# A decoder of six phases: the first pair's gathers at the start of the rotated heads moved ahead of the phase boundary

## What is computed

```
x = x + _L0_ffn_ref(_layernorm(x), ...)      # "mix": causal attention, then 8 experts, 2 per row
...
gates = softmax(x1 @ gate_w.T + gate_b)
_, top_idx = top_k(gates, 2)
expert_outputs = einsum('bsd,efd->bsef', x1, expert_w) + expert_b
moe_out = sum(sel * top_gates[..., None], axis=2)
return _layer_norm(x1 + moe_out, ln2_w, ln2_b)
...
x = x + _L1_attn_ref(_layernorm(x), ...)     # "rot": q and k through tanh layers and rotations
```

## Time and profile before

| | us |
|---|---|
| median of 3 runs (lowest, highest) | 3362.42 (3358.3, 3364.45) |
| the profiled execution, whole | 3364.29 |
| its span, first to last instruction | 3362.4 |
| mixed phase's last store, issue | 1194.56 |
| rotated heads' first instruction | 1198.15 |
| rotated heads' first matmul of rows (L2379) | 1211.6 |

### The profile page before, as it was taken

How to read it: one execution, slowest core, us unless ns; L and a number is a source line. 1 busy time by engine, 2 the same in 40 slices (tenths; PEclk the granted TensorE clock), 3 DMA queues, 4 the chain that set the end, 5 groups by cost and what they waited for, 6 DMA issues and landing times. The chain is left out here.

```text
span 3362.4 us, 71194 instructions
## 1 busy us (share of the span) xinstructions
PE 3202.7 (95%) x26568; PEld 2352.6 (70%) x26569; DVE 1772.9 (53%) x5682; ACT 1607.3 (48%) x3295; POOL 1494.3 (44%) x1990
## 2 busy tenths in 40 slices
PE   7998999998999779998999999999999999999998
PEld 5775566666777644444676777767777688999997
DVE  4666777765888556543455544554445565111114
ACT  4654666665666047884555445545455511111111
POOL 1002444433676146651665656655666564000017
PEclk9999999998999889999999999999999999999999
DMA  8700111100001650000000000000000013999963
GB/s 244 290 2 14 43 43 44 43 15 14 17 23 29 172 143 24 21 16 26 14 8 8 8 8 15 8 8 8 8 14 1 2 40 118 325 327 323 325 237 104
DMA packets 111490, 263.34 MB, mean 78 GB/s; under 512 B 24003, under 2 KB 70240, under 8 KB 95840
## 3 DMA queue, kind: packets, MB, share of 16 engines
q1 hardware_dynamic: 90208, 224.70, 21.0%
q0 software_dynamic: 16384, 26.29, 2.8%
q10 hardware_dynamic: 4608, 8.39, 0.7%
HBM read 196.61 MB, written 62.65 MB: 77 GB/s over the span
## 5 line engine op out<-in xcount | busy, mean ns | idle before, releaser
L3004 POOL TENSOR_SCALAR wide_probs<-wide_probs,wide_inverse 100x361 f32<-100x361 f32 x504 | 594.5, 1192 | 0.1
L3297 ACT ACTIVATE wide_probs<-wide_probs,wide_least 100x361 f32<-100x361 f32 x512 | 301.0, 592 | 6.8 <-DVE wide_least L3410 6.8
L3410 DVE CUSTOM_DVE_ANT_0 wide_probs<-banks,wide_bias 100x361 f32<-100x361 f32 x512 | 251.5, 529 | 42.8 <-issue 37.7
L3056 PE MATMUL banks<-w_wide_v,wide_c 64*120 64x512 f32 (+1 forms) x1152 | 266.0, 591 | 0.0
L3050 PE MATMUL banks<-wide_c,w_wide_k 64*128 64x361 f32 x1536 | 257.1, 467 | 2.3 <-PEq L4101 2.3
L2588 ACT ACTIVATE rot_h<-banks,w_rot_b 128x800 f32<-128x800 f32 x256 | 223.3, 923 | 54.7 <-PE banks L2414 49.1
L3002 POOL TENSOR_TENSOR wide_hold_pool<-eps 100x1 f32<-100x1 f32 x252 | 48.6, 193 | 444.7 <-DVE wide_inverse L3416 444.7
L3891 ACT ACTIVATE tiles_hT<-banks 128x512 f32<-128x512 f32 x114 | 68.1, 597 | 349.1 <-PE banks L3807 349.1
L3807 PEld LDWEIGHTS banks<-tiles_xT,tiles_w 128*128 128x128 f32 x1824 | 214.7, 194 | 4.7 <-issue 1.8
L3807 PE MATMUL banks<-tiles_xT,tiles_w 128*128 128x128 f32 x1824 | 215.3, 277 | 1.2 <-DVE tiles_xT L4053 1.2
L3050 PEld LDWEIGHTS banks<-wide_c,w_wide_k 64*128 64x128 f32 x1536 | 150.5, 188 | 90.8 <-issue 4.6
(11 more groups left out here) (499 smaller groups left out, 7173.2 us busy)
## 6 DMA issues: line engine op xcount, KB each, us to landing
tiles_w<-in_moe_w SPq DMA_DIRECT2D x114, 1024.0 KB, 5.2
slots<-zeros SPq DMA_DIRECT2D x58, 512.0 KB, 6.6
cross_c<-in_ctxT SPq DMA_DIRECT2D x32, 270.8 KB, 4.4
wide_c<-in_ctxT SPq DMA_DIRECT2D x32, 270.8 KB, 4.1
mix_kT<-slots SPq DMA_DIRECT2D x32, 256.0 KB, 4.3
slots<-mix_m_tiles_out ACTq DMA_DIRECT2D x32, 256.0 KB, 4.1
tiles_rows<-slots SPq DMA_DIRECT2D x57, 128.0 KB, 4.8
slots<-tiles_out SPq DMA_DIRECT2D x57, 128.0 KB, 5.0
```

The source lines that it names most:

```text
L3004: last = nc.gpsimd.tensor_scalar(t.probs[:, i, j, :], t.probs[:, i, j, :], t.inverse[:, i, j:j + 1], None, ALU.mult)
L3056: last = nc.tensor.matmul(make_bank(unit, lane)[0:kw, :], g.wide_c[rows_of(lane), of.buf, k, k0:k0 + kw], w.v[rows_of(lane), k, of.hf * BA ...
L3297: last = nc.scalar.activation(t.probs[:, i, j, :], t.probs[:, i, j, :], ACT.Exp, bias=t.least[:, i, j:j + 1], scale=-1.0, accum_out=t.rows ...
L3410: last = nc.vector.tensor_tensor_reduce(t.probs[:, i, j, :], scores(j), t.bias[:, :], -1.0, LARGEST, ALU.add, ALU.min, t.least[:, i, j:j + 1])
```

## The change

1. The four gathers of pair 0 leave GpSimd's head of the rotated heads. GpSimd issues them as its last instructions of the mixed phase, after waiting for the last store of each of the four ring places, into a buffer of its own, `first_got`.
2. On VectorE, the sums, statistics and centring of lane 0 come straight behind the tables; `base(0)` follows them.
3. The copies of the folded weights (with their waits) come behind the second statistics of pair 0, ahead of `apply_lane`; the halves of `w1` come behind `apply_lane`. PE waits for the halves (`halved`) before its first tanh layer.

```diff
@@ mix_phase, GpSimd
             tail()
+            for k in range(TILE_RING):
+                pool.wait_ge(rows_stored[k], 16 * (MIX_TILES // TILE_RING))
+            for lane in range(LANES):
+                for k in range(2):
+                    nc.gpsimd.indirect_dma_start(g.first_got[:, lane, k, :], None, g.slots[:, :],
+                                                 bass.IndirectOffsetOnAxis(ap=g.slot_i[:, 0, lane, k:k + 1], axis=0)).then_inc(g.lane_gathered[lane], 16)
@@ rotation_phase, GpSimd
             pool.wait_ge(g.loaded.rot, g.total.rot)
-            gather(0)
             root(m0, 0, 0)
@@ rotation_phase, TensorE, first_layer
                 if k == 0:
                     pe.wait_ge(s.k_kept, p + 1)
+                    if p == 0:
+                        pe.wait_ge(s.halved, 1)
@@ rotation_phase, VectorE
-            for e in range(2):
-                nc.vector.tensor_scalar(t.w1[:, e, :], w.w1[:, :], w.half[:, e:e + 1], None, ALU.mult)
-            dve.wait_ge(s.folded_ready, 1)
-            nc.vector.tensor_copy(t.w2[:, :, :, :], side[:, 0:DC * 2 * VROWS].rearrange("p (c e v) -> p c e v", e=2, v=VROWS))
-            nc.vector.tensor_copy(t.v_b[:, :], vec[:, 1:1 + DC])
-            nc.vector.tensor_copy(t.b2[:, :], vec[:, 0:1]).then_inc(s.folded, 1)
...
-            base(0)
             combine_lane(0, 0)
             centre(0, 0)
+            base(0)
             combine_lane(0, 1)
             finish(0, 0)
             centre(0, 1)
             stats_lane(0, 0)
             finish(0, 1)
             stats_lane(0, 1)
+            keep_folded()
             apply_lane(0, 0)
             apply_lane(0, 1)
+            halve_w1()
```

More of the change, by code:

```diff
@@ L2245, in rotation_phase @@
     with ExitStack() as ctx:
-        s = semaphores(nc, ctx, "rot", "fold_b masks picked own tables rot folded_ready folded turns whole_i whole near angle size cosine sine y yT_ready yT ybar mean_ready mean masked "
+        s = semaphores(nc, ctx, "rot", "fold_b halved masks picked own tables rot folded_ready folded turns whole_i whole near angle size cosine sine y yT_ready yT ybar mean_ready mean masked "
                        "k_ready k_kept q_ready q_kept kn_ready k_ends qn_ready spans inverse unit ratio rows_ready rows lane_ready proj_ready biased added "
@@ L2305, in gather @@
                     nc.gpsimd.indirect_dma_start(v.got[:, p % SETS, lane, k, :], None, g.slots[:, :],
-                                                 bass.IndirectOffsetOnAxis(ap=g.slot_i[:, p, lane, k:k + 1], axis=0)).then_inc(gathered[p % SETS] if p else lane_gathered[lane], 16)
+                                                 bass.IndirectOffsetOnAxis(ap=g.slot_i[:, p, lane, k:k + 1], axis=0)).then_inc(gathered[p % SETS], 16)
             def root(m, p, lane):
@@ L2683, in _ @@
             nc.vector.tensor_scalar(t.size[:, :, :], t.size[:, :, :], -1.0, float(np.pi / 2), ALU.mult, ALU.add).then_inc(s.size, 1)
-            for e in range(2):
-                nc.vector.tensor_scalar(t.w1[:, e, :], w.w1[:, :], w.half[:, e:e + 1], None, ALU.mult)
-            dve.wait_ge(s.folded_ready, 1)
-            nc.vector.tensor_copy(t.w2[:, :, :, :], side[:, 0:DC * 2 * VROWS].rearrange("p (c e v) -> p c e v", e=2, v=VROWS))
-            nc.vector.tensor_copy(t.v_b[:, :], vec[:, 1:1 + DC])
-            nc.vector.tensor_copy(t.b2[:, :], vec[:, 0:1]).then_inc(s.folded, 1)
-            dve.wait_ge(s.folded, 1)
-            dve.wait_ge(s.sine, 1)
-            dve.wait_ge(s.cosine, 1)
             def combine_lane(p, lane):
@@ L2702, in combine_lane @@
                 rows = v.sum[:, p % SETS, lane, :]
-                nc.vector.scalar_tensor_tensor(rows, v.got[:, p % SETS, lane, 0, :], g.coef[:, p, lane, 0:1], g.x1[:, b, :], ALU.mult, ALU.add).then_inc(s.half, 1)
+                got = v.got[:, p % SETS, lane, :, :] if p else g.first_got[:, lane, :, :]
+                nc.vector.scalar_tensor_tensor(rows, got[:, 0, :], g.coef[:, p, lane, 0:1], g.x1[:, b, :], ALU.mult, ALU.add).then_inc(s.half, 1)
                 dve.wait_ge(s.half, b + 1)
-                nc.vector.scalar_tensor_tensor(rows, v.got[:, p % SETS, lane, 1, :], g.coef[:, p, lane, 1:2], rows, ALU.mult, ALU.add).then_inc(s.summed, 1)
+                nc.vector.scalar_tensor_tensor(rows, got[:, 1, :], g.coef[:, p, lane, 1:2], rows, ALU.mult, ALU.add).then_inc(s.summed, 1)
                 dve.wait_ge(s.summed, b + 1)
@@ L2856, in step, with keep_folded, halve_w1 @@
                     ends_of_keys(k)
-            base(0)
+            def keep_folded():
+                dve.wait_ge(s.folded_ready, 1)
+                nc.vector.tensor_copy(t.w2[:, :, :, :], side[:, 0:DC * 2 * VROWS].rearrange("p (c e v) -> p c e v", e=2, v=VROWS))
+                nc.vector.tensor_copy(t.v_b[:, :], vec[:, 1:1 + DC])
+                nc.vector.tensor_copy(t.b2[:, :], vec[:, 0:1]).then_inc(s.folded, 1)
+                dve.wait_ge(s.folded, 1)
+                dve.wait_ge(s.sine, 1)
+                dve.wait_ge(s.cosine, 1)
+            def halve_w1():
+                for e in range(2):
+                    last = nc.vector.tensor_scalar(t.w1[:, e, :], w.w1[:, :], w.half[:, e:e + 1], None, ALU.mult)
+                last.then_inc(s.halved, 1)
             combine_lane(0, 0)
             centre(0, 0)
+            base(0)
             combine_lane(0, 1)
@@ L4184, in decoder @@
                 g[n] = rows_stack.enter_context(nc.sbuf_tensor("mix_" + n, shape, dt, side="right"))
+            g.first_got = rows_stack.enter_context(nc.sbuf_tensor("rot_first_got", [S, LANES, 2, D], F32, side="right"))
             mix_w["expert_b"] = weight_as(mix_stack, "mix_b", "mix_expert_b", [P, NE * D], i["mix_expert_b"].rearrange("e d -> (e d)").unsqueeze(0).broadcast_to([P, NE * D]))
```

## The result

Side by side on one chip, six runs each, the changed kernel takes 3372.91 us (3372.11 to 3377.85) and the kernel before 3363.36 us (3358.3 to 3364.45): a ratio of 1.0037, interval 1.0026 to 1.0048, so 8.7 to 16 us **slower**. The ratio, which isn't the quotient of the two medians, stands for 12.4 us; the medians themselves are 9.6 us apart (1.0028). The forecast was 3371.7 in a range of 3365 to 3376.

What follows compares the result with a forecast made beforehand. The bound was a chain of waits between mixed phase and rotated heads. Gathers 0.3 + 5.0, DRAIN 5.3, same barrier, less 0.2, gave + 10.4; less 1.15 in VectorE's head, + 9.25, a median of 3371.7 us, range 3365 to 3376.

Steps and rivals of the forecast that it cites:

- The gathers: Mixed phase's end on GpSimd: start 0.3 us after the last store lands (0.8 if slow), then 5.03 us, nothing hiding them.
- The DRAIN: GpSimd at the mixed phase's block end: paid in full behind the fourth gather, 5.3 us taken from 5.3 to 6.3.
- The rival in which it is free: Mixed phase's end: the DRAIN costs nothing, boundary 5.1 us, net + 4.0 us, time 3366.4 us; chance 0.15.
- The reason given: GpSimd's block ends: a block with indirect DMAs pays 5.3 to 6.3 us, however long ago they landed.
- The barrier: Between mixed phase and rotated heads: 1.4 us as before, VectorE starting 10.4 us later.
- all four terms: Boundary: gathers' start 0.3, gathers 5.0, DRAIN 5.3 and the same barrier, less 0.2 us, giving + 10.4 us.
- The head up to `rot_y`: VectorE's start of the rotated heads: shortened by 1.15 us, lane 1's `rot_y` 11.75 us behind the first instruction.
- The copies: VectorE ahead of `apply_lane`: 0.45 us, covered by lane 1's 0.49 us wait for GpSimd's root.
- the step "Nought": VectorE behind both lanes of `rot_y`: the products (0.61 us) moved there cost nothing.
- The cover named: VectorE behind `rot_y`: its 4.19 us wait for pair 1's rows hides the products; PE needs them 5.5 us later.
- The rival of a dip more or less: TensorE's clock after the boundary: one more or fewer drop moves the time 1.7 us, 3373.4 or 3370.0; chance 0.10.

Runs made afterwards that it cites:

- e7_waits: Changed kernel with no gathers at the mixed phase's end, GpSimd only waiting for the last stores there; one run, 3406.10 us beside 3400.41 of before.
- e3_nodrain_both: Changed kernel without GpSimd's DRAIN at the mixed phase's end and behind the clearing of semaphores; 3364.92 us over eleven runs, ratio 1.0007 to before.
- e3_nodrain_mix: Changed kernel without GpSimd's DRAIN at the end of the mixed phase's block only; 3375.34 us, ratio 1.0039 to before.
- e4_halves_front: Changed kernel with the two products of w1 back ahead of lane 0's sum; one run, 3406.32 us beside 3400.41 of before.
- e1_gathers_only: Changed kernel with VectorE's head back in its old order, only the gathers staying moved; 3374.62 us, 1.0039 times before.
- e2_head_only: Changed kernel with the four gathers back behind the barrier, VectorE's new order kept; 3366.87 us over ten runs, ratio 1.0011 to before.
- e9_two_over: Changed kernel without both GpSimd DRAINs, only lane 0's two gathers ahead of the boundary, products in front; 3396.17 us against 3393.88, ratio 1.0007.

## Why the prediction came out right, step by step

**The gathers.** They start 0.94 us behind the landing, where I took 0.3 and held 0.8 for the upper end: the bound was too low. From there to the end of the fourth it is 5.01 us (5.03 expected). Nothing hid them.

**The DRAIN.** The largest term, and the one that was only read from blocks in which it was off the path. It ended 5.62 us behind the last gather, inside the 5.3 to 6.3 given. The rival in which it is free (+ 4.0) falls with `e7_waits` (5.28 us with nothing queued), and with both DRAINs left out (`e3_nodrain_both`) the loss is gone. The reason given holds: a block with indirect DMAs pays, however long ago they landed, and `e7_waits` shows it with the scatters alone. Two things the forecast lacked: the price goes to whichever DRAIN comes first (`e3_nodrain_mix`), and it grows by 0.08 us with each indirect DMA, which is where the 0.3 above the 5.3 came from. That it needs indirect DMAs at all rests on the three blocks without them; no block was run with its own taken out.

**The barrier.** 1205.30 - 1203.94 = 1.36 us; 1.4 expected. With all four terms the boundary is 11.3 us longer than before; 10.4 was forecast, and 0.64 of the difference is the slow start, 0.3 the DRAIN.

**The head up to `rot_y`.** Better than forecast: lane 1's `rot_y` starts 10.94 us behind the first instruction instead of 11.75, a gain of 1.95 and not 1.15. The step that I had missed is the tables. I let them end as before, 3.54 us behind the first instruction, but they end at 3.08, which is 0.46 of the 0.80 us. (Most of the rest is in the joints between instructions: the sum of lane 0 starts 0.09 us ahead of the last table's end, and the additions hold lane 1's sum for 0.67 us and not 0.8.) Two small instructions on VectorE make most of the 0.46, beside gathers (kernel before) and without them (changed kernel):

```profile
1199.61 0.39 DVE L2668 TENSOR_SCALAR rot_turns<-rot_rot 128x8 f32<-128x8 f32 x1
...
1200.97 0.36 DVE L2679 TENSOR_SCALAR rot_angle<-rot_near 128x8 f32<-128x8 f32 x1
```

```profile
1206.71 0.17 DVE L2675 TENSOR_SCALAR rot_turns<-rot_rot 128x8 f32<-128x8 f32 x1
...
1207.81 0.17 DVE L2686 TENSOR_SCALAR rot_angle<-rot_near 128x8 f32<-128x8 f32 x1
```

**The copies** cost nothing, as said. In the changed kernel `rot_y` of lane 0 starts at 10.39 and lane 1's at 10.94, one 0.41 us instruction and a short wait for GpSimd's root behind it.

**The products behind `rot_y`.** Here the step "Nought" failed. The cover named was VectorE's wait of 4.19 us for pair 1's rows, and PE's weight load indeed did not wait for `halved` (1.37 us for `rot_q`, the same as in the earlier trace rows). But the wait is for gathers, and the products slowed the very gathers that VectorE then waits for: 3.05 us in place of 1.18, so 5.51 us of wait in place of 4.19. `e4_halves_front` takes the products away from there and the sum of pair 1 comes 1.28 us earlier. Of the 1.95 us won at `rot_y`, 0.10 are left at the sum of pair 1, and nothing at the 32nd tanh (63.64 us behind the first instruction, 63.62 before).

**What came through.** The two misses point the same way, and add up. The boundary costs 0.9 us more than forecast, and of the 1.15 us that the head was to give back, 0.1 are left at pair 1: + 11.2 by these landmarks, where + 9.25 was forecast. To the end of the span it is + 12.0, and the ratio stands for 12.4. The two medians happen to be only 9.6 apart, within the interval of 8.7 to 16. So it is luck that the time came out 1.2 us from the forecast; by its terms the forecast was 2 to 3 us too low. What it had right is the wait and its two large parts, the gathers in the open and the DRAIN behind them.

**The clock.** The rival of a dip more or less wasn't needed for the result, but its size can be read. TensorE's granted clock was 0.50 (1.2 GHz) from the gap until 16.0 us behind the first instruction and fell to that level twice more in the next 28 us; before, it was until 18.7, and twice. In `e1_gathers_only` it rose at 23.1 and never fell again. The prediction read the 0.88 after the gap as one such stretch that costs 1.7 us; there are two of 3.4 us each, so 0.12 of 28 us, 3.4 us, is already what they take from the clock together. The stretch from the 16th to the 32nd tanh shows what one of them is worth: 23.4 us in `e1_gathers_only` with none in it, 25.6 in the kernel before and 25.8 in the changed one with one of 3.4 us, 28.4 in `e2_head_only` with one of 6.8. A clock that differs like this from one kernel to the next moves the stage by 2 to 3 us, as much as everything that the head had to gain. It is also why I make no claim of time for `e4_halves_front`, a single run.

## What to carry to other kernels

Work moved ahead of a barrier to the engine that is done early is free only if the barrier does not wait for what that engine must still do at its end: add up its DRAIN too, even one that now ends over 70 us before the barrier (1120.75 against 1196.8 here). A price that is hidden in today's profile stands there all the same, in the row of the DRAIN against the end of the engine's last instruction. Here it is mostly the price of the 64 scatters, and GpSimd has 80 idle us behind them. In the kernel before, the DRAIN that follows the mixed phase's without new DMAs takes 47 ns (at 1197.9). So a DRAIN in the idle time would, by the 0.08 us a DMA, leave about 0.4 us to be paid behind the four gathers; that is an estimate from the table above and wasn't tried, and the 6 us until the gathers are through would stay. And before work is put into an engine's wait, ask what is being waited for, and whether the work slows just that.

## What was not expected of the hardware

- GpSimd's DRAIN at a block's end took 5.28 us with nothing queued and the last scatter over 80 us old (`e7_waits`). It grew by 0.08 us with each indirect DMA of the block (60: 4.98, 64: 5.30, 68: 5.63 us behind the last instruction) and was 0.07 us in blocks that had none. Left out at one block's end it was paid in full at the next one, 8.27 us from its begin, 5.6 behind the last gather.
- GpSimd's sequencer runs ahead of queued gathers only so far: with four of them it passed the block's end as the second started (1200.88 against 1200.85), with two 0.3 us after the first started (1198.68 against 1198.36).
- VectorE's instructions and GpSimd's gathers can slow each other: a gather took 3.05 us instead of 1.18 when VectorE's two products with four additions behind them ran beside it, in every profile in which they stood straight behind `rot_y`; and two of VectorE's 128x8 instructions took 0.36 and 0.39 us beside gathers instead of 0.17, while the others beside the same gathers kept 0.17 to 0.23. Why the products are harmless beside a gather at other places (1.01 us in the kernel before, and in `e9_two_over`) is open.
- A gather that stands behind a wait for a landing starts 0.94 us after it (1193.31 against 1192.37), not the 0.30 us that lie between two queued ones.
